# A two-layer graph network on one core: the tiles fetched row by row by SP and ACT go to GpSimd's gathers

## The reference, cut to what matters

```python
# N = 6250 nodes, 106250 edges (50000 random pairs in both directions + a loop per node),
# sorted by destination; D = 128, float32; edge_type in 0..3
h = relu(layernorm(x))
x = x + segment_sum((h @ W.T + b)[src] * edge_weight[:, None], dst)      # layer 0
h = relu(layernorm(x))
for t in range(4):                                                       # layer 1
    m = relu(concat([h[src], h[dst]]) @ W1[t] + b1[t]) @ W2[t] + b2[t]
    msgs += where(edge_type == t, m, 0)
agg = segment_sum(msgs, dst)
x = x + GRU(agg @ W_ih.T + b_ih, h @ W_hh.T + b_hh, h)
```

## Time and profile before

| | |
|---|---|
| runs | 2886.53, 2889.2, 2901.14 us |
| profiled execution, its span | 2926.7 us |
| instructions of the profile | 37042 |
| PE busy | 1325.0 us (45%) |
| VectorE (DVE) busy | 907.9 us (31%) |
| ACT busy | 567.9 us (19%) |
| POOL busy | 1530.3 us (52%), 1622 instructions |

### The profile page before, as it was taken

One profiled execution on the slowest core, in us unless ns is written; L12 is line 12 of the kernel. 1 busy time (PEld: TensorE's weight loads), 2 busy tenths in 40 slices (PEclk: granted clock), 3 DMA queues, 4 the chain that ended last, 5 costly groups with the idle time before them and its releaser, 6 DMA issues. The chain is left out here.

```text
span 2926.7 us, 37042 instructions
## 1 busy us (share of the span) xinstructions
PE 1325.0 (45%) x6646; PEld 1137.0 (39%) x6646; DVE 907.9 (31%) x2567; ACT 567.9 (19%) x1508; POOL 1530.3 (52%) x1622
## 2 busy tenths in 40 slices
PE   1333342343333433433442555556655555555657
PEld 1222232222222322322331445555555554555556
DVE  4521221212121212212221333343434334333435
ACT  3421221122212221222230111111111111111111
POOL 7465564445544644555526555555555555555551
PEclk7565665556555655555665677776777777777778
DMA  6222222222222222212222333333333333333332
GB/s 154 70 60 61 53 62 55 61 57 58 56 58 60 63 54 65 58 54 61 68 79 65 81 80 88 87 84 87 84 83 84 88 83 88 83 88 82 88 86 64
DMA packets 188009, 215.35 MB, mean 74 GB/s; under 512 B 59418, under 2 KB 134335, under 8 KB 187270
## 3 DMA queue, kind: packets, MB, share of 16 engines
q0 software_dynamic: 51488, 105.55, 14.5%
q1 hardware_dynamic: 128072, 104.79, 12.8%
q10 hardware_dynamic: 8210, 2.59, 0.4%
HBM read 176.33 MB, written 36.41 MB: 73 GB/s over the span
## 5 line engine op out<-in xcount | busy, mean ns | idle before, releaser
L1377 POOL DMA_INDIRECT accs<-h_tab,src_t x748 | 705.7, 943 | 665.5 <-PE bank L1661 388.7
L1973 PE MATMUL bank<-qwin,hotT 128*128 128x128 f32 x1662 | 318.9, 352 | 588.4 <-issue 567.7
L1661 PE MATMUL bank<-accs 128*125 128x133 f32 x1662 | 337.8, 375 | 439.4 <-ACT accs L1555 232.4
L1973 PEld LDWEIGHTS bank<-qwin,hotT 128*128 128x128 f32 x1662 | 276.2, 252 | 623.6 <-issue 603.2
L1661 PEld LDWEIGHTS bank<-accs 128*125 128x125 f32 x1662 | 314.3, 276 | 486.3 <-issue 311.3
L1788 POOL DMA_INDIRECT G<-p_tab,src_t x324 | 306.7, 947 | 288.1 <-DVE rows L1866 125.9
L1788 POOL DMA_INDIRECT edge<-p_tab,src_t x324 | 307.1, 948 | 230.5 <-DVE rows L1866 123.6
L1555 ACT ACTIVATE accs<-accs,edge 128x128 f32<-128x128 f32 x748 | 239.6, 390 | 728.4 <-issue 728.4
L1984 PE MATMUL bank<-hot,rows 128*128 128x128 f32 x1662 | 306.4, 346 | 20.4 <-ACT rows L1926 19.0
L1984 PEld LDWEIGHTS bank<-hot,rows 128*128 128x128 f32 x1662 | 288.8, 261 | 22.0 <-ACT rows L1926 19.9
L1404 DVE COPY accs<-edge 128x8 f32<-128x8 f32 x104 | 18.8, 180 | 779.9 <-PE bank L1661 535.3
(11 more groups left out here) (179 smaller groups left out, 1435.5 us busy)
## 6 DMA issues: line engine op xcount, KB each, us to landing
w1a<-p_tab ACTq DMA_DIRECT2D x1920, 0.5 KB
hotT<-h_tab SPq DMA_DIRECT2D x1802, 0.5 KB
qwin<-q_tab SPq DMA_DIRECT2D x416, 64.0 KB
hotT<-h_tab ACTq DMA_DIRECT2D x1536, 0.5 KB
w1a<-p_tab SPq DMA_DIRECT2D x1290, 0.5 KB
nodew<-key_tab SPq DMA_DIRECT2D x52, 256.0 KB
nodehot<-key_tab SPq DMA_DIRECT2D x52, 256.0 KB
accs<-h_tab,src_t POOLq DMA_INDIRECT x748
```

The source lines that it names most:

```text
L1377: eng.indirect_dma_start(slot0(o % R0)[:, t, 0:D], None, table, bass.IndirectOffsetOnAxis(src_t[:, k:k + 1], 0)).then_inc(s_g0[o % R0][t / ...
L1661: ins = eng.matmul(pb[SUM_BANK[o % 4]][0:CW, 0:FW], ones_of(o % HR)[:, t, :], slot0(o % R0)[:, t, :], start=t == 0, stop=t == last)
L1973: ins = eng.matmul(pb[2 + g % 2][:, t * D:(t + 1) * D], hotT[:, g % HT, t * P:(t + 1) * P], qwin[:, g % NG, t // PR, :], start=True, stop= ...
```

## The change

The class `ByRow`, its lists of tiles, the two tables of places with their stores (SP) and conversions (ACT), the loads of numbers, the row DMAs and the waits on them are taken out. `octet_rows` and `f1_pool` gather all 831 tiles of each layer, ACT weighs every tile from the ring, and the total of a group is one add.

```diff
-        rows_sp0 = ByRow("sp", spread(14, 6, 91, 1, TO, TO - 1) + [TAIL0],
-                         lambda j: hotT[:, 2, j % 2 * D:(j % 2 + 1) * D], hotT[0:1, 0, P:3 * P].bitcast(I32))
-        rows_sp1 = ByRow("sp", spread(10, 2, 198, 1, GT, GT - 1) + [TAIL1],
...
-        rows_act0 = ByRow("act", spread(12, 14, 180, 2, TO, TO - 2),
...
-        rows_act1 = ByRow("act", spread(15, 2, 196, 1, GT, GT - 1, [k // GT for k, _ in rows_sp1.tiles]),
...
-        def sp_row_numbers(eng):
-            for k, (tab, a) in enumerate(((place_tab0, src_i), (place_tab1, typ_i))):
-                eng.wait_ge(s["row_no"], k + 1)
-                eng.dma_start(tab.rearrange("(p e) -> p e", p=PB), a.rearrange("p g e -> p (g e)")).then_inc(s["row_st"], 16)
...
         def octet_rows(eng, o, table):
             for t in range(TO):
                 k = o * TO + t
-                if k in alone0 or k >= NTILE:
+                if k >= NTILE:
                     continue
...
             def weigh(o):
                 G0 = slot0(o % R0)
                 for h in range(2):
-                    rows0(eng, rows_act0, 2 * (o - WEIGHED0) + h)
                     eng.wait_ge(s_g0[o % R0][h], gathered0(o, h))
                     for t in range(h * GT, (h + 1) * GT):
                         k, row = o * TO + t, G0[:, t, 0:D]
                         if k >= NTILE:
                             continue
-                        if k in alone0:
-                            rows, j = alone0[k]
-                            eng.wait_ge(rows.sem[j % 2], rows.here(j))
-                            row = rows.rows_of(j)
...
             for o in range(STEPS0 + 1):
...
-                rows0(eng, rows_sp0, o)
...
                 for t in range(GT):
                     k = g * GT + t
-                    if k in alone1 or k >= NTILE:
+                    if k >= NTILE:
                         continue
...
                 if (c := chunk_at(g, U_ST)) is not None:
                     finished(c)
-                rows1(eng, rows_sp1, g)
...
-                n = next((t for t in range(GT) if g * GT + t in alone1), GT)
-                ins = eng.tensor_tensor(rows[:, g % 2, 0:n], got[:, 0:n], slot1(g % R1)[:, 0:n], ALU.add)
-                if n < GT:
-                    r_, j = alone1[g * GT + n]
-                    eng.wait_ge(r_.sem[j % 2], r_.here(j))
-                    ins = eng.tensor_tensor(rows[:, g % 2, n], got[:, n], r_.rows_of(j), ALU.add)
-                ins.then_inc(s["sum1"], 1)
+                n = min(GT, NTILE - g * GT)
+                eng.tensor_tensor(rows[:, g % 2, 0:n], got[:, 0:n], slot1(g % R1)[:, 0:n], ALU.add).then_inc(s["sum1"], 1)
...
                 if g + 1 < NGRP:
                     relu(g + 1)
-                rows1(eng, rows_act1, g)
```

More of the change, by code:

```diff
@@ L212, in gnn_program @@
         EARLY = 7
[L213 to L243, removed]
-                    u += 1
-                tiles.append((u * unit + t, shares_))
-            return tiles
@@ L255, in gnn_program @@
-        rows_act1 = ByRow("act", spread(15, 2, 196, 1, GT, GT - 1, [k // GT for k, _ in rows_sp1.tiles]),
-                          lambda j: w1a[:, 2 + j % 2, :], w1b[0:1, 2:4, :].rearrange("p a d -> p (a d)").bitcast(I32), rows_act0)
-        alone0, alone1 = ({k: (rows, j) for rows in who for j, (k, _) in enumerate(rows.tiles)}
-                          for who in ((rows_sp0, rows_act0), (rows_sp1, rows_act1)))
-        assert NTILE == NT - 1 and NTILE % GT == 3 and len({k // GT for k in alone1}) == len(alone1) == 26 and len(alone0) == 27
@@ L261, in gathered0 @@
         def gathered0(o, h):
-            return 16 * sum(o_ * TO + t not in alone0 and o_ * TO + t < NTILE
+            return 16 * sum(o_ * TO + t < NTILE
                             for o_ in range(o % R0, o + 1, R0) for t in range(h * GT, (h + 1) * GT))
         def gathered1(g):
-            return 16 * sum(g_ * GT + t not in alone1 and g_ * GT + t < NTILE for g_ in range(g % R1, g + 1, R1) for t in range(GT))
+            return 16 * sum(g_ * GT + t < NTILE for g_ in range(g % R1, g + 1, R1) for t in range(GT))
@@ L441, in row_values @@
-        def row_values(eng, rows, j, r, top):
-            a, b = j % 2 * P + r, j % 2 * P + min(r + BATCH, rows.size(j))
-            _, v = nc.values_load_multi_w_load_instructions(
-                rows.numbers[0:1, a:b], engines=[eng.engine], min_val=0, max_val=top,
-                skip_runtime_bounds_check_because="they are places of rows of the graph's edges, which the gathers read too")
-            return v
-        def row_bytes(rows, j, r):
-            return rows.rows_of(j)[r:r + 1, :].bitcast(U8)
@@ L466, in rows1 @@
-        def rows1(eng, rows, step):
-            for j, a, b in rows.at.get(step, ()):
-                rows1_part(eng, rows, j, a, b)
-        def rows1_part(eng, rows, j, a, b):
-            if a == 0:
-                eng.wait_ge(rows.known, 16 * (rows.loads + j + 1))
-                row_numbers(eng, rows, j + 1, place_tab1)
-                if j >= 2:
-                    eng.wait_ge(s["sum1"], rows.tiles[j - 2][0] // GT + 1)
-            for r in range(a, b):
-                if r % BATCH == 0:
-                    rows.held[:] = row_values(eng, rows, j, r, (N * T - 1) * ROW)
-                eng.dma_start(row_bytes(rows, j, r), p_bytes[bass.ds(rows.held[r % BATCH], ROW)].rearrange("(a d) -> a d", a=1)).then_inc(rows.sem[j % 2], 16)
@@ L2063, in _ @@
             act_wrap(eng, src4_t, 5)
[L2064 removed]
+            choose(eng, [f0_act, f1_act], [act_h0, l0_act, l1_act])
         @block.tensor
```

46 lines of the change are left out of this document (2 added, 44 removed).

## The result

The changed kernel took 2542.56 us (median of three runs, 2541.73 to 2547.53), the kernel before 2889.2: a ratio of 0.880 (95% interval 0.876 to 0.884). The same change was timed twice more in later sessions (a session is a set of kernels timed together on one chip; the expectations say "call"). There the kernel before ran some 820 us faster and the changed one some 400, and the change made it slower: 1.033 (1.031 to 1.034) and 1.034 (1.031 to 1.036). The sessions fall into two groups, called here the first condition (kernel before at 2889 to 2906 us) and the second (2065 and 2069 us).

A forecast was written before the change was run, and what follows sets the result against it. It took a chain of waits to bound the kernel, POOL's gathers, gaps and ring waits filling layer 0. Layer 0 -98, between layers -19, layer 1 -30: -147 us, span 2780, less 37.5: 2742 us; range 2640 to 2990.

The forecast's parts named there:

- +34 us: Layer 0: 27 added gathers on POOL at 1.248 us each.
- +32 us: Layer 1: 26 added gathers on POOL at 1.248 us each.
- -19 us: Between the layers: ACT may weigh the last octets from about 1468.8 us and not from 1488.0.
- -127: Layer 0's POOL ring waits: 24 units of 6.6 + 6.7 us, 319 us for 446.
- -62 us: Layer 1's POOL waits: number left at 139, each priced at 2.2 us for 2.65, 306 us for 368.5.
- 96 waits replace as many 0.3 us gaps: Layer 0: 96 POOL waits where there were 80, in place of gaps between gathers, -5 us.
- plain wait: POOL's ring wait without row DMAs in it, some 2.2 us; consumers seem to learn of releasers after POOL's run of gathers.
- low bound: Layer 1: one wait for every two of 198 groups, 99 x 2.2 = 218 us, giving -107 before the added gathers.
- where a wait ends on them: The 6548 row DMAs on SP and ACT, none on POOL or TensorE, count only at such waits.
- The rival "slower": POOL's ring waits: consumers lack pauses of POOL, not time on ACT or SP; +97 us, median 2986; chance 0.36.
- The rival "POOL bound": Both layers: POOL's waits vanish, -702 us, median 2187; chance 0.08 for below the forecast's range, on the way to it.
- The 37.5 us: Profiled execution above the median of 2889.2 (1.3%), taken as the profiler's and subtracted from 2780 to give 2742.

The follow-up runs named there:

- e4: Changed kernel with the 53 tiles neither fetched by row nor gathered, so its output is wrong: 2468.6 us.
- e12: Changed kernel with layer 1's ring of 6 groups for 10: 2527.1 us.
- e2: Kernel before with SP's row tiles gathered by POOL and rows left on ACT alone: 2672.0 us.
- e8: Changed kernel with three memsets on POOL ahead of every eighth gather in layer 1: 2491.9 us.
- e10: Changed kernel with three memsets on POOL ahead of every eighth gather in layer 1 and each octet of layer 0 from the tenth: 2493.4 us, ratio 0.863.
- e3: Kernel before with every row DMA sent and waited for, but all tiles also gathered and used from the ring: 2947.4 us.
- e1: Kernel before with ACT's row tiles gathered by POOL and rows left on SP alone: 2824.1 us.
- e18: Changed kernel timed again with a trace, in the second condition: 2139.3 us, ratio 1.0336 to the kernel before.
- e11: Changed kernel with pauses in both layers as in e10, but one memset for three: 2554.0 us, ratio 0.883.
- e14: Changed kernel with e8's pauses and layer 1's ring of 6 groups, in the second condition: 2289.5 us, ratio 1.108 to the kernel before.
- e16: Changed kernel itself, timed again in the second condition: 2132.4 us, ratio 1.0325 to the kernel before.
- e5: As e3, but each row DMA reads a fixed place, without MOVE or loads of places and registers: 2627.6 us.
- e7: All tiles gathered; one plain 64 KB DMA for each of the 53 tiles in place of 128 row DMAs, against the changed kernel: 2539.3 us.

## Why the prediction was wrong

**The sum, in the condition in which it was made.** The terms were the right ones (rows gone, POOL's waits shrink; the gathers cost their 1.25 us), the direction too; the sizes of the waits' terms were not. Of the terms, "+34 us" and "+32 us" for the gathers hold: e4 gives 73 for the two. "-19 us" between the layers measured -18. The two terms of the waits were less than half of what they should have been: -127 and -62 us forecast, some -302 (446 to 144) and -140 (368.5 to 228.4) measured. In both the same step failed: **the number of waits was kept.** The prediction took 96 waits for layer 0 ("96 waits replace as many 0.3 us gaps"), three of four at 2.2 us, and 139 for layer 1, "because a plain wait stays". A plain wait doesn't stay. It belongs to a run of gathers, not to an octet or a group, and how many octets a run spans hangs, by the timeline and e12, on how far the consumers get in its first part. With SP and ACT clear of rows they get three octets or groups through for one or two, and most runs are 24 and 12 gathers long: 37 waits of 3.89 us, 144 us in all, for the forecast 319, and 66 of 3.46, 228 us, for the forecast 306. Layer 1 came out at the low bound (-104 for -107), with 66 waits where the bound had 99; layer 0 went past its own (-255 for -206). Each wait is longer than I priced it (4.4 us behind a run of 24, 3.4 behind one of 12, 2.3 behind one of 4), and that is cheap for what it covers.

What hid this from the reading was a second step: rows were priced only "where a wait ends on them". SP's instructions aren't counted as busy and SP hardly waits, so lists of waits name mostly the engines behind it (TensorE by its "issue", VectorE by "remote"). The prediction gave SP's 1802 rows of layer 0 some 410 us of its stream, the median of the DMA alone; with MOVE and stalls they take 0.64 us each, some 1150 us. e2 shows the size: SP's rows alone are worth 223 us.

The tail, in which the prediction let nothing change but the last few row DMAs, got 9 us shorter.

**The rival "slower".** Its premise, that the pauses of POOL are what the consumers lack, is borne out in part: in layer 1 added pauses make the kernel faster (e8, 37 us), in layer 0 they don't (e10, 18 us longer). Its conclusion, that the rows therefore don't matter, fell in the first condition: the consumers need fewer pauses without rows.

**The rival "POOL bound"** is what both kernels do in the second condition. There the waits are nought before the change, the rows are free, and all that the change does is add 53 gathers: +66 forecast for that part, 67 to 70 us measured. The prediction had 2187 us for it with the 37.5 us subtracted and took it as a thing that the change could bring about; it came with the session, before the change and after it. The rule of the Trainium skill that was weighed (DMA: Bandwidth & Descriptors, "Issuing engines are not separate DMA queues"), by which the issue of the rows would be negligible and the change would only add gathers, gives +66 us. In the second condition that is within 5 us of the 67 and 70 measured; in the first the rows that it leaves out cost 406 us (e3). For the trace that I had, rejecting it was right.

**The 37.5 us.** I took the difference of profiled execution and median for the profiler's. The changed kernel's profiled span (2540.0) lies 2.6 below its median and those of e1 to e18 about 2 us below their runs, so that is no constant to be subtracted.

**What stays open.** What makes the stalls, and whether they occur at all in an execution of which no trace is taken. Both conditions were met by one chip in two sessions; within a session the runs of one kernel agree within about 1%. The instruction counts of the two traces of the kernel before are the same, their DMA packets too but for one, and the medians of a row DMA and a gather. How SP's full stream holds the rest up is in part shown, by the waits for its tiles (412 us in e1); how much more comes from the windows and stores that stand behind its rows was not tried, as no run sends the rows without waiting for them. Whether more of the pause than layer 1 took would pay in the first condition was not tried beyond e10 and e11, and whether half of SP's rows would have been enough there is not known. No kernel here is shown to beat the kernel before in both conditions. Of those with the right output, the fastest of the first are e8 and e10 (2491.9 and 2493.4), and e8 with a shorter ring, as e14, is the slowest of the second, and there the kernel before is the fastest.

## What to carry to other kernels

An engine that only issues (SP here) can set the pace without being busy and almost without waiting. Read its timeline for places where it waits; if there is none, suspect it, take its work away in an experiment, and price each instruction by what it takes beside the others' work, not at its median. When a wait is released in batches, forecast the length of the batch first and the number of waits from it. And before a small trade between engines is judged (53 gathers against 6548 row DMAs), time both kernels in more than one session: the sign of this one turned with the condition, 0.88 and 1.03.

## What the runs showed of the hardware

- In the first condition, while GpSimd issues one indirect gather after the other (944 ns and a gap of 0.3 us each), instructions on SP and ACT take now and then 0.7 or 1.4 us, MOVEs of registers (longest 1.4 us, median 0.029) as well as DMAs (longest row DMA 1.4 us, median 0.23). TensorE shows steps of that size too (weight loads of the changed kernel at 2220.15, 2220.86 and 2221.57 us; 134 of its matmuls start 0.65 to 0.78 us behind the one before, 13 in e18). Most long waits on semaphores end only behind the last gather of a run, by layer 1's medians VectorE's 1.5 us and ACT's 2.0 us behind it in the kernel before, 2.5 and 3.1 us in the changed one. In the second condition neither occurs, with the same gathers.
- In the first condition, consumers go on while GpSimd runs memsets, and mostly not while it issues gathers. Some 1.9 us of memsets ahead of every eighth gather shortened layer 1 from 1247 to 1210 us (e8). In the second condition such pauses cost what they last (layer 1 1202 us for 1042, e14 against e16).
- In the first condition, 6548 DMAs of 512 B cost this kernel 406 us with their places in registers and 86 us with fixed places (e3 and e5 against the changed kernel), at like durations of the DMAs. The same bytes in 53 DMAs of at most 64 KB cost nothing (e7).
